# Layer 1 on one Trainium2 core: the inverse root of the memory's variance as one power on GpSimd

## The reference

```python
q = _l2n((x @ Wq.T).reshape(Bs, Ts, Hs, Ds))
k = _l2n((x @ Wk.T).reshape(Bs, Ts, Hs, Ds))
v = _ln((x @ Wv.T).reshape(Bs, Ts, Hs, Ds), vn_g, vn_b)
...
b = i_gate * k * v
_, mem = jax.lax.associative_scan(comb, (a, b), axis=1)
out = _ln(mem, mn_g, mn_b) * q          # this layer norm: (mem - mean) / sqrt(var + 1e-5) * g + b
o = out.reshape(Bs * Ts, Hs, Ds)
m = o.mean(-1, keepdims=True)
var = o.var(-1, keepdims=True)
o = (o - m) / jnp.sqrt(var + 1e-05)
```

## Time and profile before

| what | value |
|---|---|
| median of 3 runs | 862.69 us (862.49 to 867.14) |
| the profiled execution's own time | 865.88 us |
| its span, first to last instruction | 864.0 us |
| outside the span in that execution | 1.88 us |
| mean granted TensorE clock | 0.938 of full |
| layer 1 begins on GpSimd (its first memset) | 610.92 us from the span's start |

### The profile page before, as it was taken

The page is one execution under the profiler, slowest core; times in us unless marked ns, Lnnn a source line. Parts: engine busy times, 40 slices in busy tenths (PEclk is TensorE's granted clock), DMA queues, the critical chain, the costliest instruction groups (busy, mean ns, idle before and its releaser), DMA issues. The chain is left out here.

```text
span 864.0 us, 15139 instructions
## 1 busy us (share of the span) xinstructions
PE 750.2 (87%) x5602; PEld 645.5 (75%) x5602; DVE 653.9 (76%) x1123; ACT 454.8 (53%) x722; POOL 420.1 (49%) x353
## 2 busy tenths in 40 slices
PE   3368799999999999999999999999568897888773
PEld 2266688888888888888888888887456686777672
DVE  6989877887777677686777777673664899998965
ACT  4246645655655655664665565565544453454411
POOL 2344444354257575667344435346354283663821
PEclk9579999999999999999999999999788899999985
DMA  5011121111001011011000000301100000000000
GB/s 156 25 38 39 38 76 44 48 36 45 20 15 38 24 47 46 20 50 27 9 21 10 12 21 3 93 3 41 48 0 1 0 1 25 1 17 10 0 25 24
DMA packets 22108, 25.88 MB, mean 30 GB/s; under 512 B 4499, under 2 KB 17171, under 8 KB 22037
## 3 DMA queue, kind: packets, MB, share of 16 engines
q1 hardware_dynamic: 22036, 24.93, 10.5%
HBM read 14.83 MB, written 3.28 MB: 21 GB/s over the span
## 5 line engine op out<-in xcount | busy, mean ns | idle before, releaser
L647 DVE TENSOR_REDUCE neg_max<-s_pair 128x4 f32<-128x1024 f32 x127 | 155.1, 1221 | 75.3 <-PE s_pair L861 75.1
L469 ACT ACTIVATE probs<-t_pair 128x1024 f32<-128x1024 f32 x128 | 131.2, 1025 | 136.8 <-PE t_pair L886 136.5
L366 POOL TENSOR_TENSOR hid<-g,hid 128x512 f32<-128x512 f32 x64 | 82.2, 1285 | 179.2 <-DVE g L758 146.1
L360 POOL TENSOR_TENSOR hid_lo<-hid,hid_hi 128x512 fp32r<-128x512 f32 x64 | 86.0, 1344 | 86.8 <-ACT hid_hi L492 86.7
L861 PE MATMUL s_pair<-K,Q 96*128 96x256 f32 x508 | 85.0, 291 | 15.6 <-DVE neg_max L647 9.2
L861 PEld LDWEIGHTS s_pair<-K,Q 96*128 96x128 f32 x508 | 75.8, 194 | 24.2 <-issue 8.1
L886 PE MATMUL t_pair<-Q,K 104*128 104x512 f32 x256 | 85.9, 417 | 0.3 <-DMA Q<-max_parts 0.3
L928 PE MATMUL down<-hi,hid_hi 128*128 128x256 f32 x256 | 84.0, 328 | 1.9 <-POOL hid_lo L360 1.9
L901 PE MATMUL misc<-probs,V 128*32 128x256 f32 x1024 | 69.2, 388 | 3.4 <-DVE kc L603 2.6
L928 PE MATMUL down<-lo,hid_hi 128*128 128x256 f32 x256 | 71.9, 281 | 0.0
L928 PE MATMUL down<-hi,hid_lo 128*128 128x256 f32 x256 | 71.7, 280 | 0.0
(11 more groups left out here) (254 smaller groups left out, 1979.5 us busy)
## 6 DMA issues: line engine op xcount, KB each, us to landing
stage<-in_ternary SPq DMA_DIRECT2D x18, 256.0 KB, 2.8
Q<-q_hi SPq DMA_DIRECT2D x64, 64.0 KB, 2.0
stage<-in_scales SPq DMA_DIRECT2D x8, 384.0 KB, 3.4
X<-in_x SPq DMA_DIRECT2D x8, 256.0 KB, 4.2
Q<-q_lo SPq DMA_DIRECT2D x32, 64.0 KB, 2.0
Q<-max_parts SPq DMA_DIRECT2D x128, 4.0 KB
out<-X SPq DMA_DIRECT2D x8, 256.0 KB, 2.1
signs<-w_stage SPq DMA_DIRECT2D x9, 128.0 KB, 1.8
```

Source lines behind the costliest of these rows:

```text
L360: pool.tensor_tensor(hid_lo[:, m % 2, :, :].rearrange("p a n -> p (a n)"), hid[:, m % 2, :], hid_hi[:, m % 2, :, :].rearrange("p a n -> p ...
L366: pool.tensor_tensor(hid[:, m % 2, :], g[:, m % 2, :], hid[:, m % 2, :], ALU.mult).then_inc(S["hid_done"], 1)
L469: act.activation(probs[:, u % 2, th, :], t_pair[:], ACT.Exp, scale=SCALE).then_inc(S["probs_done"], 1)
L647: dve.tensor_reduce(neg_max[:, u % 2, 4 * jp:4 * jp + 4], score_banks(u, jp)[:].rearrange("p (s n) -> p s n", n=SEQ), AX_X, ALU.max, negat ...
```

## The change

The nine small instructions leave VectorE. GpSimd gets two at the head of its queue in each of turns 1 to 4: one multiplies `sm` by 1 and adds the epsilon, the other raises all 128 x 64 elements to the power -0.5, in place. They are linked by a new semaphore `var_done`, and the second counts `rm_done` up. VectorE's L1524 waits for `rm_done` as before, which now comes from GpSimd. The scratch tiles `ry` and (here) `rt` are no longer used for the memory.

```diff
@@ -1034,7 +1034,7 @@
-                   stored0=16, stored1=16, roots=8, roots_late=19)
+                   stored0=16, stored1=16, roots=8, roots_late=11, var_done=1)
@@ -1218,10 +1218,18 @@
+                def memory_root():
+                    wait = waiter(pool, late)
+                    wait("sm_done", BPG)
+                    inc(pool.tensor_scalar(sm[:], sm[:], 1.0, L1_DH * EPS, ALU.mult, ALU.add), "var_done")
+                    wait("var_done", 1)
+                    inc(pool.tensor_tensor(flat(sm[:]), flat(sm[:]), half[:, 0:1].to_broadcast([P, BPG * PAIR_HEADS]), ALU.pow), "rm_done")
+
                 if late is None:
                     xn_low(pool, early, 1)
                     scaled()
                 if late is not None:
+                    memory_root()
                     memory_scaled(pool, late, 1)
@@ -1514,9 +1522,6 @@
                 def memory_normed():
                     wait = waiter(dve, late)
-                    wait("sm_done", BPG)
-                    link(dve.tensor_scalar(sm[:], sm[:], L1_DH * EPS, None, ALU.add), late, 1)
-                    inverse_root(flat(sm[:]), ry[:], rt[:], late, 1, "rm_done")
                     wait("rm_done", 1)
                     wait("o_turned", 0)
```

## The result

The changed kernel takes 898.36 us (median of 4 runs, 895.36 to 900.28) against 863.62 us for the kernel before on the same chip (4 runs, 862.49 to 867.14). The ratio is 1.0388 with a 95% interval of 1.0354 to 1.0422: slower by 30.6 to 36.4 us. The profiled execution took 899.42 us with a span of 897.5, 33.5 us more than the span before.

What follows compares the result with a forecast made beforehand. VectorE's chain through the root was taken to bound turns 1, 2 and 4, with 2.02 us of slack in turn 3. 4 x 15.6 - 9.80 = +52.6 us on the median of 862.69 gave 915, range 865 to 922.

Steps and rivals of the forecast that it cites:

- the likeliest case: GpSimd's power paid by the element, 13 to 16 us each, giving 905 to 922 us; chance 0.56.
- in between: Rival on GpSimd's power: half the extra paid once, half by the element, 8.3 us, time 886; chance 0.18.
- the sum: Delay over four turns: four powers less 9.80 us, at 15.6 us each +52.6 us.
- What bounds the place: In turns 1, 2 and 4 the chain of waits runs through VectorE's nine instructions; GpSimd idles there, 12.09 us in turn 1.
- The slack of turn 3: In turn 3 VectorE idles 2.02 us before its third feed-forward product, which comes off that turn's delay.
- The crossing and the addition: Going to GpSimd and back plus adding epsilon there: 0.72 us a turn together, apart from the power.
- The power: GpSimd's power of 64 elements a partition in each of four turns, put at 15.6 us.
- by the element: Reading of GpSimd's power row: its extra 0.49 us at two elements is all per element, 0.245 us each.
- The middle rival: GpSimd's power with its extra split evenly between once and per element: 8.3 us, time 886; chance 0.18.
- The clock: TensorE's feed-forward chunk slower after idling, 1.4 us a turn where waited for; 0 to 5.6 us over four turns.
- Not slower: Rival: GpSimd's power extra is paid once an instruction, 0.83 us, time 859.5; chance 0.22 for powers under 3.3 us.
- The wait hides: Rival: GpSimd's power runs beside other work and VectorE catches up later, 915 becoming 909; chance 0.04.

Runs made afterwards that it cites:

- half: The changed kernel with the power on 32 of 64 elements a partition, the other half's root left out: 876.37 us, ratio 1.0136 to the kernel before.
- turn3: The kernel with the power on GpSimd in turn 3 alone, VectorE's chain of nine in turns 1, 2 and 4: 870.54 us, ratio 1.0065.
- mult: The changed kernel with a multiply in place of the power, root left out so the result is wrong: 858.53 us, ratio 0.9931 to the kernel before.
- table: The changed kernel with ten more GpSimd instructions on scratch at its end, powers of 1 to 64 elements and three variants: 932.82 us in a single execution.
- warm2: The changed kernel with added TensorE matrix products during the stall, 44 in turns 1 and 2, 20 in turn 3: 895.39 us, ratio 1.0351.
- swap: The kernel before, chain of nine kept, with the next group's normalisation moved ahead of the chain in turns 1 and 2: 858.87 us, ratio 0.9928.

## Why the prediction was right, and where its size was off

The time lies in the stated range, but that range of 57 us was wide, and the likeliest case (a power of 13 to 16 us, 905 to 922 us in all, 0.56) did not come. A power of 10.54 us and a time of 898 belong to the case "in between", from 3.3 to 13 us, which had 0.18. So the path and the sum were right, and so was the direction; that the range holds the time owes something to its width.

**What bounds the place.** Right. The chain runs through the root in turns 1, 2 and 4; the idle times of 10.4 and 10.99 us in front of L1529 and half's one-to-one answer show it. GpSimd's idle time covered the start and no more.

**The slack of turn 3.** Right: 2.02 us read, and turn3 cost 4.3 to 6.9 us where 6.2 was worked out. That the ledger shows 2.10 is closer than one trace can tell, since two more traces of the changed kernel show 2.9. The idle time of 2.02 us before the third product of turn 3 is gone, as the prediction said it would be, and VectorE's busy time fell by 8.6 us where about 8 was expected.

**The crossing and the addition.** 0.08 + 0.51 + 0.09 + 0.04 were forecast. The addition took 0.25 us and not 0.51: the slope drawn from the rows at 16 and 256 elements was too steep for this shape. That is 0.26 us a turn, 1 us in all. mult, with the same crossing, came out at -6.0 us where the terms gave -5.5.

**The power.** This is the term that was mis-sized: 15.6 us forecast, 10.54 measured, 5.06 us too much in each of four turns, 20 in all. The reading "by the element" was right in kind, as the table shows, but I put nearly all of the 0.49 us on the elements. Of those 0.49, the line puts 0.15 on what is paid once (0.36 less the 0.21 of a call) and 0.32 on two elements. The reason given, that the 0.21 of a plain operation already holds all that is paid once, is the step that failed: a power pays about 0.15 us more. Two elements are a poor place to read a slope from: that 0.15 us, which can't be told apart there, is multiplied by 32 at 64 elements. The middle rival with its even split, 8.3 us and 886, was nearer than my value, and the truth lies between the two.

**The clock.** Left out of the sum and put at 0 to 5.6 us in the range. Behind the stalls it is 1.6 us over turns 1 and 2 by the traces of warm2 and of the changed kernel next to it; 2.7 us if the slow output products at the end of turn 2 are counted too. The pair of rows from which I took 1.4 us is no clean one: after the same 2.00 us of idling the same chunk took 3.48 us in one trace of the changed kernel and 2.14 in another, so the idle time just ahead does not settle its length.

**The sum with the measured terms.** 4 x 10.54 - 9.80 - 4 x 0.26 = 31.3; with 1.5 us of waits behind the slow chunks in turns 1 and 2 (0.52, 0.51 and 0.50 us), 32.8. The span grew by 33.5; the 0.7 that is left is no more than what VectorE's waits for the output products differ by from trace to trace.

**The rivals.** The power by halves, "in between", is what came, with 10.54 us for its 8.3. "Not slower", the power paid once, is refuted by the table. Its arithmetic for the case that the power is nearly free was sound: mult shows it. "The wait hides" found nothing beyond turn 3.

**The Trainium skill's figures.** The table has 159 ns for an element of the power. The Trainium skill, "GPSIMD Engine Reference", section "Elementwise — side-by-side cycle accounting", has about 2.6 cycles of 1.2 GHz an element for plain two-input operations and about 12 with data-dependent branches. The 159 ns would be an estimated 191 such cycles, so neither figure prices a power. The 2.1 ns of the plain rows agree with the first; the same tile multiplied took 0.29 us, too short to tell a price by the element.

## What to carry to other kernels

The power here has a price by the element that a small shape hides; measure such a function at the size at which it will run before moving work there, or at least at two sizes, since one point can't part what is paid once from what is paid each time. A chain of nine short instructions (2.27 us for 64 elements) can be far cheaper than the one instruction that replaces it (10.54 us). And where VectorE's work is slowed beside GpSimd's multiplications, moving it into GpSimd's idle time can pay as much as taking instructions away: swap came out 6.2 us under the kernel before, and mult, which takes the nine instructions off VectorE, 6.0.

## What the runs showed of the hardware

A power on GpSimd cost 0.36 us and 159 ns for each element of a partition (table), the same for 16 and for 128 partitions.

Four normalising instructions of VectorE took 1.38 us beside the power and beside an idle GpSimd, but 4.36 us beside GpSimd's multiplications of 128 x 512. I had expected the power to hold them off too. The Trainium skill, "SBUF — State Buffer", section "Who interferes with whom", calls the port pair that the two engines share an exclusive lock which the first to start keeps for its whole instruction. The multiplications agree with that: in turn 1 of the changed kernel the first of the four took 0.41 us and the other three 1.35 to 1.42, while GpSimd's three multiplications ran at 1.26 to 1.36 us each. The power, which would have held the four back for 10 us, does not. The other way round a power was held up once in layer 0: of the eight at L327 in the kernel before, seven took 0.69 to 0.72 us, and the one beside VectorE's L707, a two-input instruction of 128 x 768, took 1.40. Whether L707 is the cause was not tried.

TensorE's chunk of eight products took 3.78 us after 8.64 us of idling, 3.78 after 2.97 us of idling behind 32 products, 2.11 after 1.39 us behind 32, and 2.14 after 0.33 us behind 44. After 2.00 us of idling it took 3.48 us in one execution and 2.14 in another of the same kernel.
